# A fused cross-attention and expert-mixed FFN kernel: value vectors mixed by one small product per token, with operands turned by DMA through DRAM

## The reference, cut to what matters

```python
gate_v = jnp.einsum('btc,hec->bthe', x, Ws)
w, sel = jax.lax.top_k(gate_v, K)                  # K = 2
mix_v = jnp.einsum('bthk,bthke->bthe', sigmoid(w), one_hot(sel, E))
proj_v = jnp.einsum('btc,edc->bted', x, Wv)        # 8 experts x 64 values for each token
v = jnp.einsum('bthe,bted->bhtd', mix_v, proj_v)   # 16 heads x 64 values for each token
probs = softmax((q * scale) @ k)                   # per head, 56 x 56
attn = jnp.einsum('bhij,bhjd->bihd', probs, v)
mask_o = one_hot(top_k(gate_o, K)).sum(axis=3)
res = jnp.einsum('bthe,bthd,efd->bthf', mask_o, attn, Wo).sum(axis=2)
```

## Time and profile before

| | |
|---|---|
| median of 3 runs | 469.22 us (467.35 to 471.89) |
| profiled execution | 469.56 us, of which 467.7 us lie between its first and last instruction |
| mean granted TensorE clock | 0.973 |
| scores of pair 1 and of pair 15 start at | 217.14 us and 445.54 us |
| one iteration in the loop | 16.3 us |

### The profile page before, as it was taken

The page is one execution under the profiler, slowest core; times in us unless marked ns, Lnnn a source line. Parts: engine busy times, 40 slices in busy tenths (PEclk is TensorE's granted clock), DMA queues, the critical chain, the costliest instruction groups (busy, mean ns, idle before and its releaser), DMA issues.

```text
span 467.7 us, 25765 instructions
## 1 busy us (share of the span) xinstructions
PE 412.8 (88%) x10859; PEld 359.2 (77%) x10859; DVE 404.1 (86%) x775; ACT 337.7 (72%) x924; POOL 133.6 (29%) x142
## 2 busy tenths in 40 slices
PE   1877999999999986578999999999999999999985
PEld 1666789889889875557878788787878878787874
DVE  6897788998989943779999999999999999999962
ACT  6585788788788653366776697688769767876872
POOL 7645788889888650000000000000000000000000
PEclk9999999999999987598999999999999999999999
DMA  7972965465460000000000000000000000000000
GB/s 174 362 239 78 281 208 201 139 204 196 136 202 0 1 4 1 1 1 5 3 7 0 5 5 5 0 5 5 0 5 5 5 0 5 5 2 2 8 8 13
DMA packets 18158, 29.51 MB, mean 63 GB/s; under 512 B 3017, under 2 KB 14025, under 8 KB 18121
## 3 DMA queue, kind: packets, MB, share of 16 engines
q1 hardware_dynamic: 18120, 28.97, 19.5%
HBM read 28.05 MB, written 0.92 MB: 62 GB/s over the span
## 4 chain that ended last, share of the span: by engine, by line
DVE 41%; PE 30%; ACT 13%; issue 12%; DMA 2%; SPq 1%; DVEq 1%; ACTq 0%
DVE ctxf_all L960 9%; DVE ctxf_all L934 6%; PE ps L1062 5%; DVE attnf L971 4%; ACT pf L511 4%; DVE ah L988 4%; PE ps L1296 2%; PE ps L1095 2%; PE ps L1109 2%; ACT e_sb L609 2%; PE ps L1110 2%; PE ps L1111 2%; ACT p L514 2%; PE ps L1077 2%; ACT ctxT L505 2%
## 5 line engine op out<-in xcount | busy, mean ns | idle before, releaser
L609 ACT ACTIVATE e_sb<-ps,smn 128x56 f32<-128x56 f32 x256 | 76.4, 374 | 0.4 <-DVE smn L978 0.4
L609 ACT ACTIVATION_READ_ACCUMULATOR e_sb<-ps,smn 128x1 f32 x256 | 67.2, 274 | 0.0
L960 DVE TENSOR_TENSOR ctxf_all<-mixp,diag_h 128x3584 f16<-128x3584 f16 x32 | 63.2, 2017 | 0.0
L391 POOL TENSOR_TENSOR nat<-ctxf_all,nat 128x640 f16<-128x640 f32 x32 | 55.0, 1719 | 22.8 <-ACT nat L500 22.7
L1062 PE MATMUL ps<-ident,nat 128*128 128x128 f16 x768 | 56.7, 223 | 5.3 <-DVE ctxT L736 2.8
L397 POOL TENSOR_TENSOR p<-pf,p 128x672 f16<-128x672 f32 x32 | 55.3, 1728 | 18.9 <-ACT p L514 18.8
L1062 PEld LDWEIGHTS ps<-ident,nat 128*128 128x128 f16 x768 | 45.0, 99 | 8.1 <-issue 6.5
L500 ACT CAST nat<-ctxf_all 128x1536 f16<-128x1536 f32 x32 | 47.5, 1483 | 4.0 <-DMA ctxf_all<-in_ctx_dram 2.9
L736 DVE COPY ctxT<-ps 128x1024 f16<-128x1024 f16 x64 | 42.3, 681 | 1.7 <-PE ps L1062 1.7
L511 ACT ACTIVATE pf<-ps 128x672 f32<-128x672 f32 x32 | 23.7, 740 | 25.6 <-PE ps L1095 25.6
L1231 PE MATMUL ps<-xn,mT 128*128 128x112 f16 x256 | 41.1, 219 | 0.0
(11 more groups left out here) (172 smaller groups left out, 1235.0 us busy)
## 6 DMA issues: line engine op xcount, KB each, us to landing
ctxf_all<-in_ctx_dram SPq DMA_DIRECT2D x32, 704.0 KB
ctxf_all<-in_ctx_dram SPq DMA_DIRECT2D x32, 46.0 KB
x_all<-in_x_dram SPq DMA_DIRECT2D x4, 224.0 KB
out_dram<-y_all SPq DMA_DIRECT2D x32, 28.0 KB
ctxf_all<-in_ctx_dram SPq DMA_DIRECT2D x32, 18.0 KB
fwq_nat<-in_L_ffn_Wq_dram SPq DMA_DIRECT2D x1, 512.0 KB, 6.2
fwk_nat<-in_L_ffn_Wk_dram SPq DMA_DIRECT2D x1, 512.0 KB, 6.1
fwv_nat<-in_L_ffn_Wv_dram SPq DMA_DIRECT2D x1, 256.0 KB, 5.9
```

Source lines behind the costliest of these rows:

```text
L391: pool.tensor_tensor(nat[k][:, 1, 7 * C:], ctxf[k][:, 7 * C:], nat[k][:, 0, 7 * C:], ALU.subtract).then_inc(natlo2, 1)
L609: last = act.activation(e_sb[:, k, b, 0:S], ps[:, b, S * k:S * k + S], ACT.Exp, bias=smn[:, K16 * b + k:K16 * b + k + 1], scale=-1.0, accu ...
L960: last = dve.tensor_tensor(dv[:, part, :, :, :], mixp[:, part, :, :].unsqueeze(2).broadcast_to((P, 2 * NQ, HALF, H)), diag_h[:, :, :].unsq ...
```

## The change

The block matrix and everything that feeds it go: `diag_h`, `mixp`, `pj`, `dv`, the products L1296, the splits L636, L955, L626, L951, L960 and the 48 products L1259. The projections become one product of 112 tokens with all 8 experts (tokens on partitions), and the mix weights are computed with tokens on partitions too, by one 128-wide product for the value gates. ACT writes the projections and DVE the mix weights into one tile `st` with 8 x 80 numbers per token. SP writes `st` to a scratch tensor in DRAM, waits for it, and reads it back with four DMAs into `tok`, experts on partitions and tokens along the row, one quarter of the tokens on partitions 0, 32, 64 and 96 onwards. PE then makes one fp32 product per token, 112 a pair, with 8 rows, 64 columns and 16 moving columns. The values, now 64-row blocks, are turned with 32 fp32 products where 8 transposes stood.

All four streams are written in a new order: within an iteration PE now starts with the scores of pair i and does the value part of the same pair behind them; the z products of the next pair are split around the transposes.

```diff
+        st = ctxf_all[:, n_dm:n_dm + n_st].rearrange("p (e c) -> p e c", e=E)
+        tok = ctxf_all[:, n_dm + n_st:n_dm + n_st + n_u].rearrange("p (t c) -> p t c", t=HALF)
+        st_dram = nc.dram_tensor("by_token", [2 * S, E, DP], F32).ap()
...
+            def by_token(i):
+
+                after(sp, f_pje, i + 1)
+                after(sp, f_mix, i + 1)
+                after(sp, d_tok, 16 * NQ * i)
+                sp.dma_start(st_dram[:, :, :], st[0:2 * S, :, :]).then_inc(d_st, 16)
+                after(sp, f_vt, i)
+                after(sp, d_st, 16 * i + 16)
+                for q in range(NQ):
+                    sp.dma_start(tok[32 * q:32 * q + E, :, :],
+                                 st_dram[HALF * q:HALF * q + HALF, :, :].rearrange("t e c -> e t c")).then_inc(d_tok, 16)
...
-                    for part in range(2):
-                        if part == 1:
-                            dve.wait_ge(f_ml, i + 1)
-                        last = dve.tensor_tensor(dv[:, part, :, :, :],
-                                                 mixp[:, part, :, :].unsqueeze(2).broadcast_to((P, 2 * NQ, HALF, H)),
-                                                 diag_h[:, :, :].unsqueeze(1).broadcast_to((P, 2 * NQ, HALF, H)), ALU.mult)
-                    last.then_inc(f_d, 1)
...
+            def token_values(i):
+
+                after(pe, d_tok, 16 * NQ * (i + 1))
+                after(pe, f_nrm, 2 * i)
+                for t in range(HALF):
                     for q in range(NQ):
...
+                        b, r = q // 2, slice(32 * q, 32 * q + E)
+                        last = pe.matmul(ps[DH * b:DH * b + DH, 6 + q % 2, H * t:H * t + H], tok[r, t, 0:DH], tok[r, t, DH:DP],
+                                         start=True, stop=True)
+                last.then_inc(f_vt, 1)
...
+            def values_turn(i):
...
+                for h in range(H):
+                    for b in range(2):
+                        r = slice(SLOT * b, SLOT * b + SLOT)
+                        last = pe.matmul(ps[r, 4 + h // 8, DH * (h % 8):DH * (h % 8) + DH], vT[r, h, :], ident[r, r], start=True, stop=True)
+                last.then_inc(f_vv, 1)
...
+            def projections(i):
...
+                pe.matmul(ps[:, 3, :], xnT[:, :], fwvT[:, :, :].rearrange("p e d -> p (e d)"), start=True, stop=True).then_inc(f_pj, 1)
...
+            def proj_evac(i):
+
+                after(act, f_pj, i + 1)
+                after(act, d_st, 16 * i)
+                act.copy(st[:, :, 0:DH], ps[:, 3, :].rearrange("p (e d) -> p e d", e=E)).then_inc(f_pje, 1)
```

More of the change, by code:

```diff
@@ L176, in xattn_ffn @@
         d_out = sem("d_out")
+        d_st = sem("d_st")
+        d_tok = sem("d_tok")
         c_zero = sem("c_zero")
@@ L360, in _ @@
                                  y_all[SLOT * b:SLOT * b + S, bass.ds(i * C, C)]).then_inc(d_out, 16)
+            by_token(0)
+            by_token(1)
+            by_token(2)
+            with sp.Fori(0, NP - 3) as i:
+                store(i)
+                by_token(i + 3)
+            for i in range(NP - 3, NP):
+                store(i)
             sp.wait_ge(d_out, 32 * NP)
@@ L1010, in _ @@
+            for i in range(NP - 1, NP + 1):
+                iteration(i)
         @block.tensor
@@ new lines, in scores @@
+            def scores(i):
+                after(pe, f_z1e, i + 1)
+                after(pe, f_z2e, i + 1)
+                for q in range(NQ):
+                    b = q // 2
+                    for h4 in range(4):
+                        last = pe.matmul(ps[32 * h4:32 * h4 + 32, b, 224 * (q % 2):224 * (q % 2) + 224].rearrange("p (n j) -> p n j", j=S),
+                                         xnT[:, HALF * q:HALF * q + 32], z[:, h4::4, S * b:S * b + S], start=True, stop=True)
+                last.then_inc(f_s, 1)
@@ new lines, in output @@
+            def output(i):
+                after(pe, f_ae, i + 1)
+                after(pe, f_pje, min(i + 3, NP) if isinstance(i, int) else i + 3)
+                after(pe, f_y, i)
+                pe.matmul(ps[:, 3, 0:C], ident[:, :], x_all[:, bass.ds(i * C, C)], start=True, stop=False)
+                for j in range(E // 2):
+                    last = pe.matmul(ps[:, 3, 0:C], aT[:, j, :, :].rearrange("p b t -> p (b t)"), wo2[:, j, :],
+                                     start=False, stop=(j == E // 2 - 1))
+                last.then_inc(f_o, 1)
@@ new lines, in iteration @@
+            def iteration(i):
+                if has(i):
+                    scores(i)
+                if has(i + 1):
+                    xn_turn(i + 1)
+                if has(i - 2):
+                    output(i - 2)
+                if has(i + 1):
+                    gates(i + 1)
+                if has(i):
+                    token_values(i)
+                if has(i - 1):
+                    attended(i - 1)
+                if has(i + 1):
+                    after(pe, f_xh, i + 2)
+                    after(pe, f_xl, i + 2)
+                    after(pe, f_ge, i + 2)
+                    after(pe, f_pje, i + 1)
+                    after(pe, f_y, i - 1)
+                    z_heads(8, 2).then_inc(f_z2, 1)
+                if has(i):
+                    exps_turn(i)
+                    values_turn(i)
+                if has(i + 1):
+                    projections(i + 1)
+                    after(pe, f_ete, i + 1)
+                    z_heads(0, 0).then_inc(f_z1, 1)
+                if has(i):
+                    probs_values(i)
```

429 lines of the change are left out of this document (173 added, 256 removed).

## The result

The changed kernel takes 605.08 us (median of 4 runs, 602.73 to 610.44); the kernel before takes 468.69 us beside it. The ratio is 1.291, 95% interval 1.280 to 1.303. It is slower, as forecast, but by 136 us and not by 15: the forecast of 484 us and its whole range, up to 508, are too low.

A forecast was written before the change was run, and what follows sets the result against it. DVE set the pace with PE close behind; PE would become the bound at 17.45 us an iteration against 16.31. 14 iterations gave +16.0, start -4.5, end +2.2: +13.7 on 469.56, so 484 us, range 465 to 508.

The forecast's parts named there:

- PE's work, full clock, no wait: Sum of PE's lost and gained work in one FFN iteration: 16.97 us against 16.31 before, making PE the bound.
- W, the write: SP's store of `st` to DRAM, from ACT's copy until it lands: 2.3 us (1.9 to 3.3).
- R, the read, up to PE's start: The four loads of `by_token` from DRAM before L1289: 4.1 us (3.4 to 4.9).
- cover of the trip: PE's work between projections and value products, 6.7 us less 0.9 for the copy: 5.8 us of W + R hidden.
- stall: PE's wait for the loads before L1289 each iteration: 0.5 us (0 to 2.4), making an iteration 17.45.
- start, end: Outside the 14 loop steps: pair 1's scores come 4.5 us sooner, pair 15's final product 2.2 us later.
- the 4.8 us off DVE: DVE's stretch from L951 to L971's start goes, 4.8 us an iteration, but buys nothing because PE becomes the bound.
- 15 ns a record: Price of the 224 records in PE's token products: 0.06 us for a round of four, 3.4 us in all.
- The rival with a floor of 25 to 30 ns: Each small product at L1289 costs at least that: 5.6 to 6.5 us, total 515 us; chance 0.11.
- Eight engines for each load: Each of the four loads of 8 experts goes over 8 DMA engines at most, not 16.
- I take 2.7: Time in us for reading 896 pieces, chosen between 3.5 by pieces, 2.2 by size and 2.0 for four issues.
- The long-trip rival (8 us or more): The DRAM round trip is slow through SP or DRAM: 19.3 us an iteration, 510 us; chance 0.10.

The follow-up runs named there:

- the spread rows: Changed kernel with the experts' rows read back to every fourth partition, zeros between, each token product multiplying 32 rows: 566.6 us.
- the table of spans: Spans of changed-kernel variants: large products without wait 481.6 us, with wait 566.8; token products without wait 510.2, with wait 608.6.
- one trip: Changed kernel with only pair 0 making the DRAM round trip: 512.1 us; with 18 large products replacing the token products as well: 483.4 us.
- the early order: Changed kernel with projections right behind the token products and DVE mixing before making masks: 525.4 us; with fp16 records 482.3 us.
- the one with less idle time on PE: Early order, fp16 records, with ACT's copies of turned values and projections and the gates' tanh ahead of its second exponentials: 487.1 us.

## Why the prediction was wrong

| term | forecast | measured |
|---|---|---|
| PE's work, full clock, no wait | 16.97 us | 16.89 |
| token products, full clock | 3.4 | 3.45 (5.9 on average in the changed kernel) |
| transposes of the values | 1.95 | 2.01 |
| W, the write | 2.3 | 2.6 |
| R, the read, up to PE's start | 4.1 | 6.85 |
| cover of the trip | 5.8 | 2.6 + 6.85 - 3.55 = 5.9 |
| stall | 0.5 | 3.7 |
| clock | 0 | 25.17 - 16.89 - 3.7 = 4.6 |
| start, end | -4.5, +2.2 | +7.4, +9.5 |

**What held.** PE becomes the bound, and the 4.8 us off DVE buy nothing: it held; DVE is busy for 54% of the span. The sum on PE held to 0.1 us, and the choice in it that mattered, 15 ns a record from L1320, L1242 and L1296, held as well: 3.45 / 224 is 15.4 ns. The rival with a floor of 25 to 30 ns fell, and with it the 25 ns of the Trainium skill ("TensorE: Matmul & The Clock Gate", "Wait — 56ns, not 53.3ns?"), for products that run beside each other on blocks of the array; in fp16 they are 1.07 / 112 = 9.6 ns apart. Eight engines for each load held: 928 packets are 896 pieces and 32 signals, eight a load.

**The first step that failed is R.** "I take 2.7" for the 896 pieces stood between two prices per piece. They took 4.45 us, from 327.37 to 331.82, and the cause, shown by the spread rows, is one that I had not priced: all pieces land on few groups of partitions. I took the rate of loads whose rows covered 56 partitions. The rest of R was short too: 0.9 us from the first issue to the first piece and 1.5 from the last piece to PE's start are 2.4 us, where I had 1.4 from the stores. With the rows spread, the last of these fell to 0.5. The long-trip rival (8 us or more) named the right term, at 9.4 us. I put it at 0.10 and gave SP or DRAM as the cause.

**The second, and the larger, is one that the sum doesn't contain.** Every duration was taken at the clock of the earlier trace rows, 1.00, and no step asked if the new instructions and the new wait would keep it. By the table of spans the order itself, with one trip, costs 481.6 - 467.7 = 14 us over the kernel before. That this is the size of the forecast is chance: the forecast had 17.45 us an iteration and 2.3 us off at start and end, this run has 17.04 and 3.7 us on. The trip's standing still costs 59.0 - 5.2 = 54 more, and the clock the rest, 73 of 141. In the iteration shown the half-clock part falls on L1289 and L1304, on the engine that sets the pace. My rivals each added one price to an iteration; none could reach 25 us. One of their prices was off as well: with 5.6 us for the 224 records the sum gives 17.45 + 2.2 = 19.65 an iteration and 514 us, not 510.

**Start and end** failed for the same two reasons, and the start for a third. The first token products started at 208.67, where I had 201.2, and took 6.17 us, as did the last ones. Of these 7.5 us, 4.0 are the trip, 10.4 in place of 6.4. The other 3.4 passed before it: I had let it start with the mix weights, at 194.8, but the write went out at 198.25. The FFN stage began some 2.4 us later than before, so that the mix weights were ready at 197.55, and ACT's copy of the projections came later still. They stand behind the first z products on PE and ran at the lower clock (2.05 us, against 1.12 for the same product at full clock at 345.64):

```profile
195.56 2.05 PE L1334 MATMUL ps<-fwvT,xnT 128*128 128x512 f32 x2 [1.10 <-ACT xn1T L658]
```

What stays open: why the same iteration keeps the clock in one stretch and not in the next; which property of the small products counts, beyond rows and columns together; and why the early order kept it with fp16 records while the one with less idle time on PE did not.

## What to carry to other kernels

When a change puts a wait or a stretch of small products on the engine that sets the pace, price its clock as well as its time: take durations from rows at both levels, and give the fall a chance of its own. For a DMA whose destination covers few partitions, take the rate from a row that covers as few, or spread the rows. The product per token paid here only in fp16, and only with the values' transposes in fp16 too; in fp32, at 3.45 us of 17, no order tried here made it pay.

## What the runs showed that I had not expected

- Products of 16 and of 64 moving columns, of 8 and of 32 rows, took the same time on four blocks of the array: 3.45 to 3.49 us for 224.
- A large product among products on blocks took 0.16 us, in a row of its like 0.058.
- A load whose destination steps over partitions took longer to issue: 2.81 us for four against 1.47.
- In the run with 32 rows and 64 columns, the token products of pairs 1 to 3 took 4.6 to 5.7 us at a clock of 1.00, with pauses up to 1.65 us inside that nothing in the profile explains; they are gone from the second turn of the loop (pair 4) on. The other runs with one trip that keep the small products have such pauses among those pairs too, up to 1.96 us.
